# Attention, adapters and a large FFN on one core: the causal mask of the row maxima, split into constant rows and quarter-width products

## The chip, the core and the metric

The kernel runs on one core of a Trainium2 chip. The metric is the time of one execution on the device in microseconds (us), the median of several runs. The core has five engines with a queue of instructions each: TensorE (PE, with its weight loads written PEld), VectorE (DVE), ScalarE (ACT), GpSimd (POOL) and SyncE (SP), which here only issues DMAs. They meet at semaphores alone.

## What is computed

16 sequences of 256 tokens with 256 features go through two residual blocks: x + attention(adapter(x)), and x + ffn(cond2(x)). The change touches the attention only:

```python
q = (x @ Wq.T).reshape(b, t, NUM_HEADS, HEAD_DIM)      # 16 heads of 16
k = x @ Wk.T                                           # one key head for all
v = x @ Wv.T
logits = jnp.einsum('btnh,bsh->bnts', q, k) * scale
mask = (q_pos >= k_pos) & (q_pos <= k_pos + WINDOW)    # WINDOW = 256 >= t
masked = jnp.where(mask[None, None, :, :], logits, -1e30)
probs = jax.nn.softmax(masked, axis=-1)
out = jnp.einsum('bnts,bsh->btnh', probs, v).reshape(b, t, WIDTH)
return out @ Wf.T + bf
```

Softmax subtracts the maximum of each row of `masked`, so the kernel needs, for each query and head, the maximum over the keys up to its own token. After it come an FFN block with experts chosen per sequence and a second, ternary FFN.

## The kernel before

There are three phases: attention (one sequence an iteration, to about 353 us of the trace), the expert FFN, and the ternary FFN, in which PE streams 512-column products without a pause (line 1599). The change is in the attention alone.

**The iteration.** Each engine runs the same list of steps, written out by hand in a function `iteration`, and a loop repeats it. Three sequences are in work at once: while iteration b does scores and exponentials of sequence b, it also does the adapter, norm, queries and keys of sequence b+2 (`front`), the row maxima of sequence b+1 (`maxima`), and the products with the values, the output projection and the residual of sequence b-1 (`tail`). Operands of three sequences lie in three slots: `q_t[slot]` (128 rows x 8 pairs of heads x 256 tokens) and `keys[slot]` (128 rows x 2 x 256). In a slot rows 0 to 63 serve the even head of a pair and rows 64 to 127 the odd one; of the 64, rows 0 to 47 hold the query's high part, rest and high part against the key's high, high and low part, and rows 48 and 49 the row maximum against -1. Rows 50 to 63 are zero on the query side.

**The maxima.** `max_scores(n, slot, u)` makes unit u of the 12 units of a sequence on PE (line 1282 the products of queries and keys, line 1285 the mask), and `maximum` on DVE (line 927) reduces the 512 columns of its bank to the negated maxima. Units 0 to 3 take tokens 0 to 127 and two pairs of heads each (two products of 256 columns, then a mask product of 512 columns); units 4 to 11 take tokens 128 to 255 and one pair (one product of 512 columns, then a mask product of 256 columns, which covers the last 128 keys). The mask product multiplies a bf16 identity of 128 x 128 by a constant bf16 tile with -1e30 above the diagonal and adds it into the bank. Two banks alternate, so unit u waits for the reduction of unit u-2.

**What follows on PE.** Between the units stand the score products (`scores`, line 1301, 512 columns each, read by ACT's exponential, line 624), transposes (1237, 1340, 1347), projections (1248, 1258, 1356), and the adapter (1218, 1228). The exponentials are masked on POOL (`causal`, line 521). The products with the values (`products`, lines 1320 and 1322) have 32 rows of output each: four of them, to output rows 0, 32, 64 and 96 of a bank, stand one behind the other, with fp32 operands, of which the trace has two records per product.

**The end of an iteration.** On DVE: the reductions of units 10 and 11, the split of the maxima (941, 943), the residual (959), then values and low keys (920, 906). On PE: units 10 and 11, the output projection (1356), two transposes of the values (1264), the transposes of the maxima (1290), scores 10 and 11, and then the next iteration's `adapter_in` (1218), whose bank the residual on DVE reads.

**The start.** POOL clears the three `q_t` slots and other constants (lines 495 to 504). SP issues the loads of constants, the first loads of sequence 1 (`load_front(1)`), then `move_queries(0, 0)` (line 321, six DMAs that put the parts of the queries on their rows), and so on.

Of the kernel before, what the change touches and what calls it, by code (L numbers as in the profile page):

```python
# [26 lines left out]
SLOTS = 3  # L27

# [74 lines left out]
def build(nc, x_t, x_tok, lang, expert, cond_w1, cond_w2, cond_vec, w_q, w_kv, w_f, b_f, ident_d, mask_d, key_row_d,  # L103
          fc1_w, fc1_b, fc2_w, fc2_b, exp_w, exp_b, ffn_d, hid_d, ffn_s, out_t):
    ctx = ExitStack()
    with ctx:
# [40 lines left out]
        for name in """  # L147
                warm_made sp_settled pool_settled dve_settled raw_loaded const_loaded ffn_copied ffn_loaded const_made ident_made row_made
                front_loaded hidden_mm hidden_out adapted_mm u_out norm_t_mm norm_t_out q_mm q_hi q_low q_moved kv_mm keys_hi keys_out kv_out v_t_mm values_out
                stats_ready moments_ready veps_ready rstd_ready norm_ready  # L150
                max_mm max_out m2_hi m2_ready max_t_mm max_t_out maxima_moved
                score_mm exp_done masked early_mm early_out late_mm late_out
                pv_t_mm recip_done att_out att_t_mm att_t_out proj_mm x1_out resid_loaded x1_stored
                phase2_over fc1_hi_made fc1_split fc2_loaded fc2_hi_made fc2_split
                xa_loaded xa_hi xa_split expert_loaded expert_hi expert_split bias_loaded
                unit_mm raw_ready hi_ready act_ready y_ready y_stored
                comb_made comb_checked comb_stored low_step bits_max bits_summed flag_ready
                yc_loaded yc_hi yc_split resid2_loaded sil_ready prod_ready in_mm h_mm w3_part out_mm
                op_hi op_ready p1_out t1_ready t2_ready t3_ready t4_ready u2_ready u3_ready
                x11_ready c21_ready x21_ready c22_ready x22_ready c12_ready x12_ready  # L160
                out_ready out_stored""".split():
            s[name] = sem(name)
# [100 lines left out]

        block = ctx.enter_context(nc.Block())
# [22 lines left out]
        def _(sp):  # L287
# [21 lines left out]
            def load_resid(b):  # L309
                if not is_first(b):  # L310
                    sp.wait_ge(s["x1_out"], HEAD + KD * b)
                sp.dma_start(resid[:, :, :], x_t[:, :, bass.ds(b * T, T)]).then_inc(s["resid_loaded"], 16)

# [83 lines left out]
            sp.dma_start(key_row[:, :], key_row_d).then_inc(s["const_loaded"], 16)  # L397
            load_resid(0)
# [5 lines left out]
            sp.wait_ge(s["const_made"], 1)  # L404
            move_queries(0, 0)
            load_front(2)
            sp.wait_ge(s["const_made"], 3)
# [83 lines left out]
        def _(pool):  # L491
# [3 lines left out]
            nc.gpsimd.memset(q_t[0][:, :, :].bitcast(F32), 0.0).then_inc(s["const_made"], 1)  # L495
            nc.gpsimd.memset(half[:, :], -0.5).then_inc(s["const_made"], 1)
            nc.gpsimd.memset(q_t[1][:, :, :].bitcast(F32), 0.0).then_inc(s["const_made"], 1)
            for slot in range(SLOTS):
                nc.gpsimd.memset(values[slot][:, :, :], 0.0).then_inc(s["const_made"], 1)
            pool.wait_ge(s["const_made"], 3 + SLOTS)  # L500
            for slot in range(SLOTS):
                nc.gpsimd.memset(values[slot][:, :, HD:HD + 1], 1.0).then_inc(s["const_made"], 1)
            nc.gpsimd.memset(q_t[2][:, :, :].bitcast(F32), 0.0).then_inc(s["const_made"], 1)
            nc.gpsimd.memset(ones[:, :], 1.0).then_inc(s["const_made"], 1)
# [3 lines left out]
            def rstd_of(n):  # L508
                pool.wait_ge(s["veps_ready"], n + 1)
                if is_first(n):  # L510
                    pool.wait_ge(s["const_made"], 2)
                nc.gpsimd.tensor_tensor(rstd[:, :], veps[:, :], half[:, :], ALU.pow).then_inc(s["rstd_ready"], 1)
# [76 lines left out]
        def _(act):  # L589
# [23 lines left out]
            def keys_high(n, slot):  # L613
                act.wait_ge(s["kv_out"], n + 1)
                for par in range(2):
                    nc.scalar.activation(keys[slot][:, par, :], kv[:, :], ACT.Identity,
                                         bias=key_row[:, 2 * par:2 * par + 1], scale=key_row[:, 2 * par + 1:2 * par + 2]).then_inc(s["keys_hi"], 1)
# [264 lines left out]
        def _(dve):  # L882
# [20 lines left out]
            def keys_low(n, slot):  # L903
                dve.wait_ge(s["keys_hi"], 2 * (n + 1))
                for par, rows in enumerate((slice(32, 64), slice(96, 128))):
                    nc.vector.tensor_tensor(keys[slot][rows, par, :], kv[rows, :], keys[slot][rows, par, :].bitcast(F32),
                                            ALU.subtract).then_inc(s["keys_out"], 1)
# [6 lines left out]
            def values_of(n, slot):  # L914
                dve.wait_ge(s["v_t_mm"], n + 1)
                if n in (0, 1, 2) if isinstance(n, int) else False:
                    dve.wait_ge(s["const_made"], 3 + 2 * SLOTS)
# [134 lines left out]
            dve.wait_ge(s["front_loaded"], 80)  # L1052
            add_adapted(0)
# [154 lines left out]
        def _(pe):  # L1208
# [58 lines left out]
            def max_scores(n, slot, u):  # L1267
# [3 lines left out]
                if u == 0:  # L1271
                    pe.wait_ge(s["q_moved"], 96 * (n + 1))
                    pe.wait_ge(s["keys_out"], 2 * (n + 1))
                    if not is_first(n):
# [10 lines left out]
                mm(diag, ident_b[:, :], mask[:, 0:2 * pairs, :], start=False, stop=True).then_inc(s["max_mm"], 1)  # L1285
# [433 lines left out]
```

## Time and profile before

| | us |
|---|---|
| median of 3 runs | 1143.06 |
| lowest, highest | 1142.23, 1147.89 |
| the profiled execution's own time | 1147.46 |
| its span, first to last instruction | 1145.7 |

All rows come from one profiled execution. A row of a group of instructions gives line, engine, operation, output<-inputs, `weights` shape, the moving operand's shape and type, count, then busy time and the mean duration (ns) of one, and the idle time ahead of them with what ended it. A row of a timeline gives start and length in us, and how many records were merged. A matmul's length holds the way through the array too: the next one starts well before it ends, so the pace of PE is read from the distance between starts. Some mask products have no record (176 of 192).

### The profile page before, as it was taken

To read this page: it belongs to the slowest core of one execution; us is meant where nothing else is said; L and a number is where in the kernel's file an instruction comes from. 1 tells how busy PE (TensorE), PEld (TensorE's weight loads), DVE (VectorE), ACT (ScalarE), POOL (GpSimd) and SP (SyncE) were. 2 spreads that over 40 slices of the span, in tenths; PEclk is the share of its full clock that TensorE was granted. 3 is DMA by queue.
4 is the path that set the end of the run, shared out by engine and by line. 5 is a ranking of instruction groups with operands and counts; after the bars stand their busy time and mean duration, and the time that the engine had idled before them with its cause. 6 is when DMAs were issued, how large, how long until landed. Compare 5 with 4: busy or idle time off the path is not lost.

```text
span 1145.7 us, 17992 instructions
## 1 busy us (share of the span) xinstructions
PE 1103.2 (96%) x5947; PEld 869.3 (76%) x5963; DVE 783.1 (68%) x1377; ACT 589.5 (51%) x990; POOL 173.4 (15%) x192
## 2 busy tenths in 40 slices
PE   5697999999998999999999999999999999999998
PEld 3465777676765888888888888888888888888886
DVE  2565777777776567566487775777757787568875
ACT  1154656565656445434365654656545564455653
POOL 2021222222245443541000000000000000000000
PEclk9688999999999999999999999999999999999999
DMA  4455555546474456545414443144430444404421
GB/s 134 68 150 171 106 101 101 100 101 103 99 205 148 166 200 210 214 174 185 155 41 164 165 147 110 37 165 147 164 111 11 164 142 162 144 0 147 147 92 38
DMA packets 80591, 148.57 MB, mean 130 GB/s; under 512 B 15328, under 2 KB 41840, under 8 KB 80368
## 3 DMA queue, kind: packets, MB, share of 16 engines
q1 hardware_dynamic: 71026, 126.92, 38.8%
q10 hardware_dynamic: 9518, 21.11, 5.2%
q8 instruction: 19, 0.31, 0.1%
q14 instruction: 28, 0.23, 0.1%
HBM read 107.63 MB, written 30.41 MB: 120 GB/s over the span
## 4 chain that ended last, share of the span: by engine, by line
PE 91%; DVE 3%; DMA 1%; ACT 1%; SPq 1%; issue 1%; ACTq 0%; POOL 0%; DVEq 0%; POOLq 0%
PE bank L1599 35%; PE bank L1561 10%; PE bank L1364 7%; PE bank L1611 5%; PE bank L1282 4%; PE bank L1537 4%; PE bank L1531 4%; PE bank L1301 3%; PE bank L1248 3%; PE bank L1320 2%; PE bank L1356 2%; PE bank L1285 2%; PE bank L1218 2%; DMA vec<-in_cond_vec 1%; PE bank L1228 1%; PE bank L1258 1%
## 5 line engine op out<-in xcount | busy, mean ns | idle before, releaser
L1599 PE MATMUL bank<-op_hi,w_ring 128*128 128x512 f32 x896 | 348.7, 389 | 0.0
L1599 PE MATMUL bank<-op_lo,w_ring 128*128 128x512 f32 x896 | 348.6, 389 | 0.0
L1118 DVE TENSOR_TENSOR op_lo<-x_blk,op_hi 128x512 fp32r<-128x512 f32 x288 | 193.4, 683 | 30.4 <-ACT op_hi L805 30.3
L805 ACT ACTIVATE op_hi<-x_blk 128x512 fp32r<-128x512 f32 x288 | 162.8, 620 | 73.5 <-PE bank L1599 69.3
L1599 PEld LDWEIGHTS bank<-op_lo,w_ring 128*128 128x128 f32 x896 | 168.2, 188 | 35.0
L1599 PEld LDWEIGHTS bank<-op_hi,w_ring 128*128 128x128 f32 x896 | 168.1, 188 | 35.0
L927 DVE TENSOR_REDUCE neg_max<-bank 128x2 f32<-128x512 f32 (+1 forms) x192 | 124.8, 684 | 35.7 <-PE bank L1285 34.4
L624 ACT ACTIVATE p<-bank 128x512 f32<-128x512 f32 x192 | 108.7, 596 | 39.0 <-PE bank L1301 34.7
L829 ACT ACTIVATE x_blk<-x_blk,scales 128x512 f32<-128x512 f32 x96 | 69.3, 722 | 67.0 <-DVE x_blk L1171 28.9
L1561 PE MATMUL bank<-tile_hi,ffn_w 128*128 128x512 f32 x256 | 101.6, 397 | 0.0
L1561 PE MATMUL bank<-tile_lo,ffn_w 128*128 128x512 f32 x256 | 100.9, 394 | 0.0
L521 POOL TENSOR_SCALAR_AFFINE_SELECT p<-p 128x512 f32<-128x512 f32 (+1 forms) x96 | 75.9, 791 | 162.6 <-ACT p L624 162.5
L1301 PE MATMUL bank<-q_t,keys 128*128 128x512 f32 x192 | 94.0, 505 | 0.6 <-ACT p L624 0.6
L757 ACT ACTIVATE g_raw<-bank,fc_bias 128x512 f32<-128x512 f32 x64 | 44.0, 689 | 91.8 <-PE bank L1364 77.6
L1282 PE MATMUL bank<-keys,q_t 128*128 128x256 f32 (+1 forms) x256 | 85.9, 392 | 2.6 <-DVE neg_max L927 2.5
L817 ACT ACTIVATE sil<-bank,scales 128x512 f32<-128x512 f32 x64 | 43.9, 688 | 79.2 <-PE bank L1561 79.1
L1126 DVE SCALAR_TENSOR_TENSOR x_blk<-bank,scales,sil 128x512 f32<-128x512 f32 x64 | 48.1, 751 | 51.9 <-PE bank L1561 49.8
L1282 PEld LDWEIGHTS bank<-keys,q_t 128*128 128x128 f32 x256 | 49.7, 199 | 11.1 <-DVE neg_max L927 5.5
L562 POOL TENSOR_TENSOR comb<-comb 128x512 f32<-128x512 f32 x32 | 49.5, 1546 | 56.5 <-DVE g_parts L1084 55.0
L1561 PEld LDWEIGHTS bank<-tile_hi,ffn_w 128*128 128x128 f32 x256 | 48.1, 188 | 11.9
L1561 PEld LDWEIGHTS bank<-tile_lo,ffn_w 128*128 128x128 f32 x256 | 48.2, 188 | 11.2
L1285 PE MATMUL bank<-mask,ident_b 128*128 128x256 bf16 (+1 forms) x176 | 56.6, 322 | 0.0
(126 smaller groups left out, 1741.4 us busy)
## 6 DMA issues: line engine op xcount, KB each, us to landing
w_ring<-hid_scratch SPq DMA_DIRECT2D x112, 512.0 KB, 4.6
hid_scratch<-comb ACTq DMA_DIRECT2D x8, 1792.0 KB, 7.8
q_t<-q_high SPq DMA_DIRECT2D x64, 128.0 KB, 4.9
comb<-in_hid_d ACTq DMA_DIRECT2D x6, 768.0 KB, 5.1
xt<-in_x_t SPq DMA_DIRECT2D x16, 256.0 KB
xtok<-in_x_tok SPq DMA_DIRECT2D x16, 256.0 KB
resid<-in_x_t SPq DMA_DIRECT2D x16, 256.0 KB, 3.0
q_t<-q_rest SPq DMA_DIRECT2D x32, 128.0 KB, 4.6
```

Source lines behind the costliest of these rows:

```text
L521: nc.gpsimd.affine_select(out=v, in_=v, compare_op=ALU.is_ge, fill=0.0, base=0, pattern=[[0, v.shape[1]], [1, P]], channel_multiplier=-1). ...
L624: nc.scalar.activation(dst.rearrange("p c t -> p (c t)"), score_bank[par][:, :], ACT.Exp).then_inc(s["exp_done"], 1)
L805: nc.scalar.activation(op_hi[:, o % OP_RING, k], x_blk[:, operand_home(o), k], ACT.Copy).then_inc(s["op_hi"], 1)
L829: nc.scalar.activation(x_blk[:, at[block], m], src, ACT.Gelu, scale=sc[:, KB * row + m:KB * row + m + 1]).then_inc(s[made], 1)
L927: nc.vector.tensor_reduce(neg_max[:, t, first:first + pairs, :].rearrange("p c a -> p (c a)"), max_bank[u % 2][:, :].rearrange("p (c k) -> ...
L1118: nc.vector.tensor_tensor(op_lo[:, o % OP_RING, k], x_blk[:, operand_home(o), k], op_hi[:, o % OP_RING, k].bitcast(F32), ALU.subtract).the ...
L1282: mm(dst[:, 2 * c * seen:2 * (c + 1) * seen].rearrange("p (a k) -> p a k", a=2), q_t[slot][:, first + c, t * P:(t + 1) * P], keys[slot][:, ...
L1285: mm(diag, ident_b[:, :], mask[:, 0:2 * pairs, :], start=False, stop=True).then_inc(s["max_mm"], 1)
L1301: mm(score_bank[par][:, :].rearrange("p (c t) -> p c t", c=pairs), keys[slot][:, par, k0:k0 + P], q_t[slot][:, first:first + pairs, q0:T], ...
L1364: last = mm(bank, w[:, k, cols], v[:, k, :], start=i == 0, stop=i == len(passes) - 1)
L1561: last = mm(bank, w_at(at, k, HID, m), read(v[:, half, k, :]), start=k == 0 and v is yc_hi, stop=k == KD - 1 and v is yc_lo)
L1599: last = mm(banks[first_bank + m][:, :], w, read(v[:, q % OP_RING, k, :]), start=k == 0 and v is op_hi and i not in (P2, P3), stop=k == KB ...
```

## The change

The mask of the maxima is made in two parts.

Between blocks of 32 tokens: rows 50 to 56 of every `q_t` slot and `keys` slot become seven constant rows. Row r of the queries is 1 where the token's block is below r, row r of the keys is -1e30 where the key's block is r, so the ordinary product of queries and keys adds -1e30 for every key in a later block. They are loaded once (`rank_d`), rounded on DVE and copied into the three slots by six DMAs. POOL clears the `keys` slots too, and `keys_high` (ACT) and `keys_low` (DVE) write no longer over these rows.

Within a block of 32: the one mask product with 128 output rows becomes four, each with 32 weight columns of the identity, 32 output rows, and the 32 keys of that block for each head: 4 x 128 columns for units 0 to 3 (before: 512), 4 x 64 for units 4 to 11 (before: 256). The diff, cut to its core:

```diff
+BLOCK = 32
+RANKS = T // BLOCK - 1
+MASK_ROW = MAX_ROW + 2
...
+        rank_raw, rank = x1[0:RANKS, :, :], att_t[0:RANKS, :, :]
...
+            def move_ranks(slot):
+
+                sp.wait_ge(s["rank_made"], 1)
+                rows = slice(MASK_ROW, MASK_ROW + RANKS)
+                for to, part, count in ((q_t, 0, NP), (keys, 1, 2)):
+                    sp.dma_start(to[slot][rows, :, :].bitcast(F32),
+                                 rank[:, part, :].rearrange("p (c t) -> p c t", c=1).broadcast_to([RANKS, count, T])).then_inc(s["ranks_moved"], 16)
...
             sp.dma_start(key_row[:, :], key_row_d).then_inc(s["const_loaded"], 16)
+            sp.dma_start(rank_raw, rank_d).then_inc(s["rank_loaded"], 16)
             load_resid(0)
...
             load_front(1)
-            sp.wait_ge(s["const_made"], 1)
+            sp.wait_ge(s["const_made"], 7 + 2 * SLOTS)
+            for slot in range(SLOTS):
+                move_ranks(slot)
             move_queries(0, 0)
             load_front(2)
-            sp.wait_ge(s["const_made"], 3)
             move_queries(1, 1)
...
             nc.gpsimd.memset(q_t[0][:, :, :].bitcast(F32), 0.0).then_inc(s["const_made"], 1)
+            nc.gpsimd.memset(keys[0][:, :, :].bitcast(F32), 0.0).then_inc(s["const_made"], 1)
...
                 for par in range(2):
-                    nc.scalar.activation(keys[slot][:, par, :], kv[:, :], ACT.Identity,
-                                         bias=key_row[:, 2 * par:2 * par + 1], scale=key_row[:, 2 * par + 1:2 * par + 2]).then_inc(s["keys_hi"], 1)
+                    rows = slice(SLOT * par, SLOT * par + MASK_ROW)
+                    nc.scalar.activation(keys[slot][rows, par, :], kv[rows, :], ACT.Identity,
+                                         bias=key_row[rows, 2 * par:2 * par + 1], scale=key_row[rows, 2 * par + 1:2 * par + 2]).then_inc(s["keys_hi"], 1)
...
-                for par, rows in enumerate((slice(32, 64), slice(96, 128))):
+                for par, rows in enumerate((slice(32, MASK_ROW), slice(SLOT + 32, SLOT + MASK_ROW))):
...
             dve.wait_ge(s["front_loaded"], 80)
+            dve.wait_ge(s["rank_loaded"], 16)
+            nc.vector.tensor_copy(rank.bitcast(F32R), rank_raw).then_inc(s["rank_made"], 1)
             add_adapted(0)
...
                     pe.wait_ge(s["keys_out"], 2 * (n + 1))
+                    if is_first(n):
+                        pe.wait_ge(s["ranks_moved"], 32 * SLOTS)
...
                 diag = dst[:, :].rearrange("p (h k) -> p h k", k=seen)[:, :, seen - P:seen]
-                mm(diag, ident_b[:, :], mask[:, 0:2 * pairs, :], start=False, stop=True).then_inc(s["max_mm"], 1)
+                for at in range(0, P, BLOCK):
+                    own = slice(at, at + BLOCK)
+                    last = mm(diag[own, :, own], ident_b[:, own], mask[:, 0:2 * pairs, own], start=False, stop=True)
+                last.then_inc(s["max_mm"], 1)
...
+    block, r = np.arange(T) // BLOCK, np.arange(1, RANKS + 1)[:, None]
+    a["rank_d"] = np.stack([np.where(block < r, 1.0, 0.0), np.where(block == r, -1e30, 0.0)], 1).astype(np.float32)
```

On PE, in the loop of the attention, around units 4 to 6 (line 1301 or 1328 is a score product). Before:

```order
L1282 MATMUL bank<-keys,q_t 128x512 [waits max_out]
L1285 MATMUL bank<-mask,ident_b 128x2x128
L1298 REGISTER_ALU
L1301 MATMUL bank<-q_t,keys 128x512 [waits exp_done]
L1279 REGISTER_ALU
L1282 MATMUL bank<-keys,q_t 128x512 [waits max_out]
L1285 MATMUL bank<-mask,ident_b 128x2x128
L1248 MATMUL bank<-norm_t,wq 128x256 [waits late_out,norm_t_out]
```

The same place after the change:

```order
L1306 MATMUL bank<-keys,q_t 128x512 [waits max_out]
L1311 MATMUL bank<-mask,ident_b 32x2x32 x4
L1325 REGISTER_ALU
L1328 MATMUL bank<-q_t,keys 128x512 [waits exp_done]
L1303 REGISTER_ALU
L1306 MATMUL bank<-keys,q_t 128x512 [waits max_out]
L1311 MATMUL bank<-mask,ident_b 32x2x32 x4
L1270 MATMUL bank<-norm_t,wq 128x256 [waits late_out,norm_t_out]
```

The order of the steps stays; one full-width mask product has become four quarter-width ones at every unit.

On SP's queue at the start, behind the loads of sequence 1, before the change:

```order
L301 DMA xtok<-in_x_tok 128x512 [waits u_out,norm_t_out]
L302 ISA
L302 DMA vec<-in_cond_vec 128x5
L321 DMA q_t<-q_high 16x8x256 [waits const_made,q_low]
L321 DMA q_t<-q_high 16x8x256
```

After it:

```order
L307 DMA xtok<-in_x_tok 128x512 [waits u_out,norm_t_out]
L308 ISA
L308 DMA vec<-in_cond_vec 128x5
L325 DMA q_t<-att_t 7x8x256 [waits rank_made,const_made]
L325 DMA keys<-att_t 7x2x256
L325 DMA q_t<-att_t 7x8x256 [waits rank_made]
L325 DMA keys<-att_t 7x2x256
L325 DMA q_t<-att_t 7x8x256 [waits rank_made]
L325 DMA keys<-att_t 7x2x256
L335 DMA q_t<-q_high 16x8x256 [waits q_low]
L335 DMA q_t<-q_high 16x8x256
```

Six DMAs now stand ahead of the queries of sequence 0.

## Rows read from the trace of the kernel before

**Rows 1.** The page: its head, and the group of mask products from its part 5.
```profile
span 1145.7 us, 17992 instructions
...
L1285 PE MATMUL bank<-mask,ident_b 128*128 128x256 bf16 (+1 forms) x176 | 56.6, 322 | 0.0
```

**Rows 2.** Stretches: length; busy of PE, PEld, DVE, ACT, POOL; granted clock; DMA; GB/s.
```profile
40.00:60.00 20.00, 15.62 (x48) 9.12 (x47) 13.80 (x28) 2.62 (x6) 0.33 (x1) 0.67 0.32 42
...
200.00:300.00 100.00, 99.48 (x764) 70.65 (x767) 73.52 (x169) 59.84 (x119) 27.54 (x36) 1.00 0.55 102
```

**Rows 3.** Timeline of PE: the first maxima products of two iterations in a row.
```profile
206.57 0.97 PE L1282 MATMUL bank<-keys,q_t 128*128 128x256 f32 x4
...
226.28 0.97 PE L1282 MATMUL bank<-keys,q_t 128*128 128x256 f32 x4
```

**Rows 4.** Timeline of PE around two mask products of 512 and 256 columns.
```profile
209.64 0.40 PE L1282 MATMUL bank<-keys,q_t 128*128 128x256 f32 x2
...
210.34 0.27 PE L1237 MATMUL bank<-ident,norm 128*128 128x128 f32 x1
...
211.02 0.39 PE L1282 MATMUL bank<-keys,q_t 128*128 128x512 f32 x1
...
211.60 0.39 PE L1282 MATMUL bank<-keys,q_t 128*128 128x512 f32 x1
```

**Rows 5.** Timeline of PE: back-to-back 512-column products of the FFN, first and seventh.
```profile
820.06 0.39 PE L1599 MATMUL bank<-op_hi,w_ring 128*128 128x512 f32 x1
...
821.42 0.39 PE L1599 MATMUL bank<-op_hi,w_ring 128*128 128x512 f32 x1
```

**Rows 6.** Timelines of PE and its weight loads, from full-width products to quarter-width ones and back.
```profile
202.32 0.38 PE L1218 MATMUL bank<-xt,w1c 128*128 128x256 f32 x1
...
202.63 0.16 PEld L1320 LDWEIGHTS bank<-p,values 128*32 128x32 f32 x8 [0.33 <-issue]
...
202.87 0.40 PE L1320 MATMUL bank<-p,values 128*32 128x256 f32 x4
203.09 0.40 PE L1322 MATMUL bank<-p,values 128*32 128x128 f32 x8
203.31 0.40 PE L1320 MATMUL bank<-p,values 128*32 128x256 f32 x4
...
203.86 0.28 PE L1322 MATMUL bank<-p,values 128*32 128x128 f32 x2
...
204.07 0.30 PEld L1228 LDWEIGHTS bank<-w2c,h_t 65*128 65x128 f32 x2 [0.20 <-issue]
...
204.39 0.38 PE L1228 MATMUL bank<-w2c,h_t 65*128 65x256 f32 x1
```

**Rows 7.** The end of an iteration: timelines of DVE, PE, PEld; then L1218's idle by releaser.
```profile
218.18 1.29 DVE L927 TENSOR_REDUCE neg_max<-bank 128x2 f32<-128x512 f32 x2 [0.34 <-PE bank L1285]
...
220.35 0.88 DVE L959 SCALAR_TENSOR_TENSOR x<-bank,bf,resid 128x256 f32<-128x256 f32 x2
...
218.22 0.28 PE L1285 MATMUL bank<-mask,ident_b 128*128 128x256 bf16 x1
...
220.47 0.71 PE L1301 MATMUL bank<-q_t,keys 128*128 128x512 f32 x2
...
221.28 0.51 PEld L1218 LDWEIGHTS bank<-xt,w1c 128*128 128x128 f32 x3 [0.53 <-DVE x L959]
...
  DVE x L959: 5.6, 11
```

**Rows 8.** The start: timelines of DVE, SP's queue (SPq) and POOL.
```profile
14.40 0.69 DVE L886 TENSOR_TENSOR u<-bank,xtok 128x512 f32<-128x512 f32 x1 [12.27 <-PE bank L1228]
...
20.96 0.34 SPq L302 DMA_DIRECT2D vec<-in_cond_vec  x1
25.52 1.31 SPq L321 DMA_DIRECT2D q_t<-q_high  x2
...
5.82 1.80 POOL L503 MEMSET q_t<- 128x2048 f32 x1
```

More of the change, by code:

```diff
@@ L100, in score_fill, with build @@
     return 2 * [0, 1, None, 2, 3][f], 2, 0, 0
-def build(nc, x_t, x_tok, lang, expert, cond_w1, cond_w2, cond_vec, w_q, w_kv, w_f, b_f, ident_d, mask_d, key_row_d,
+def build(nc, x_t, x_tok, lang, expert, cond_w1, cond_w2, cond_vec, w_q, w_kv, w_f, b_f, ident_d, mask_d, key_row_d, rank_d,
           fc1_w, fc1_b, fc2_w, fc2_b, exp_w, exp_b, ffn_d, hid_d, ffn_s, out_t):
@@ L147, in build @@
         for name in """
-                warm_made sp_settled pool_settled dve_settled raw_loaded const_loaded ffn_copied ffn_loaded const_made ident_made row_made
+                warm_made sp_settled pool_settled dve_settled raw_loaded const_loaded rank_loaded rank_made ranks_moved ffn_copied ffn_loaded const_made ident_made row_made
                 front_loaded hidden_mm hidden_out adapted_mm u_out norm_t_mm norm_t_out q_mm q_hi q_low q_moved kv_mm keys_hi keys_out kv_out v_t_mm values_out
@@ L495, in _ @@
             nc.gpsimd.memset(q_t[0][:, :, :].bitcast(F32), 0.0).then_inc(s["const_made"], 1)
+            nc.gpsimd.memset(keys[0][:, :, :].bitcast(F32), 0.0).then_inc(s["const_made"], 1)
             nc.gpsimd.memset(half[:, :], -0.5).then_inc(s["const_made"], 1)
             nc.gpsimd.memset(q_t[1][:, :, :].bitcast(F32), 0.0).then_inc(s["const_made"], 1)
+            nc.gpsimd.memset(keys[1][:, :, :].bitcast(F32), 0.0).then_inc(s["const_made"], 1)
             for slot in range(SLOTS):
                 nc.gpsimd.memset(values[slot][:, :, :], 0.0).then_inc(s["const_made"], 1)
-            pool.wait_ge(s["const_made"], 3 + SLOTS)
+            pool.wait_ge(s["const_made"], 5 + SLOTS)
             for slot in range(SLOTS):
@@ L503, in _ @@
             nc.gpsimd.memset(q_t[2][:, :, :].bitcast(F32), 0.0).then_inc(s["const_made"], 1)
+            nc.gpsimd.memset(keys[2][:, :, :].bitcast(F32), 0.0).then_inc(s["const_made"], 1)
             nc.gpsimd.memset(ones[:, :], 1.0).then_inc(s["const_made"], 1)
@@ L510, in rstd_of @@
                 if is_first(n):
-                    pool.wait_ge(s["const_made"], 2)
+                    pool.wait_ge(s["const_made"], 3)
                 nc.gpsimd.tensor_tensor(rstd[:, :], veps[:, :], half[:, :], ALU.pow).then_inc(s["rstd_ready"], 1)
@@ L916, in values_of @@
                 if n in (0, 1, 2) if isinstance(n, int) else False:
-                    dve.wait_ge(s["const_made"], 3 + 2 * SLOTS)
+                    dve.wait_ge(s["const_made"], 5 + 2 * SLOTS)
                 src, at = ring[1][:, T:2 * T].rearrange("p (t c) -> p t c", t=NT), 0
```

## The prediction

> **What bounds the kernel now.** I read the busy time by stretch first. In a hundred microseconds of the attention PE is busy for 99.5 us at a granted clock of 1.00 (the level of 2.4 GHz), DVE for 73.5 and ACT for 59.8 [rows 2]: PE sets the time there, and what it does less or more shows in the total, unless PE was waiting anyway. Busy time alone hides such waits, because the length of a matmul record holds its way through the array, so I then read the distances between starts in the timeline. One iteration is 226.28 - 206.57 = 19.71 us [rows 3]. The mask products count as 56.6 us busy [rows 1], but that is not what they cost, since their records lie over their neighbours'.
>
> What one costs is in [rows 4]. From one 512-column maxima product to the next stand a product, a mask product of 256 columns and a score product of 512: 211.60 - 211.02 = 0.58 us. Products of 512 columns alone come every (821.42 - 820.06) / 6 = 0.227 us [rows 5]. So the mask product of 256 columns costs 0.58 - 2 x 0.227 = 0.13. For the 512-column mask: 210.34 - 209.64 = 0.70 us for two products of 256 columns (together 0.23), the mask and a score product (0.227), which leaves 0.24. An iteration has 8 of the one and 4 of the other: 8 x 0.13 + 4 x 0.24 = 2.0 us, and 16 sequences 32 us. This is all that the masks can give back.
>
> **The quarter-width products.** The trace has products with 32 output rows to four different quarters of a bank: those with the values. Two things can be read from them [rows 6].
>
> First, four of them run at once. The first pass of four with 128 columns starts at 203.09, the next four with 256 columns at 203.31; between lie two passes of 128 columns for all four quarters, eight records, in 0.22 us, so 0.11 for four. The four with 256 columns before them (202.87 to 203.09) take 0.22, which is what one such fp32 pass takes alone. And four records together last 0.40 us (start 203.31) where one lasts 0.38 (start 202.32): the four starts are spread over 0.02 us.
>
> Second, going in and out is not free. The last full-width pass ahead of the quarters starts at 202.32, and the second round of the quarters at 202.87. At 0.22 us a pass, two passes would be 0.43 us; it is 0.55. **Entering costs 0.12 us.** The weight loader sat idle for 0.33 us before the quarters [rows 6], though its wait was for nothing that the profile shows ("issue"), where elsewhere it loads under the running product. The last round of quarters starts up to 203.86 (two records) and takes 0.11, so it is through at 203.97; the second full-width pass of the next product starts at 204.39, its first one therefore counts from 204.39 - 0.22 = 204.17. **Leaving costs 0.20 us**, again with an idle weight loader (0.20, "issue"). The three other crossings of this iteration that I looked at have the same two distances to the hundredth, so these are no late semaphores but a price of changing between full and quarter width: the running products have to be through before the new weights are loaded, and the load is then uncovered.
>
> The Trainium skill says so too, in "TensorEngine Tiling (Array Packing)", Key Properties: changing the tiling mode drains TensorE. This trace agrees (the loader's 0.33 and 0.20 us), and the page gives no figure for it. Against it stands the span model of "TensorE: Matmul & The Clock Gate", Part 3 (measured speedup vs the span model), by which four tiles take the time of one and about 4 ns for each further one, with no word of a drain; by that rule alone the change would end as the first rival below does.
>
> **The sum.** After the change every unit crosses twice: its query-key product is full width, the four quarters are not, and what follows is full width again. The order of the steps puts no two masks side by side. The streaming of the quarters is small: 256 more bf16 columns cost 0.24 - 0.13 = 0.11, so 64 columns cost 0.03 and 128 columns 0.05, all four at once, and 0.02 for the spread of their starts. A mask then costs
> - units 4 to 11: 0.12 + 0.03 + 0.02 + 0.20 = 0.37, before 0.13: +0.24;
> - units 0 to 3: 0.12 + 0.05 + 0.02 + 0.20 = 0.39, before 0.24: +0.15.
>
> The pace of 0.227 holds some 0.01 beyond the streaming (two fp32 passes of 256 columns take 0.22), and a drain that begins at the end of the stream has it already; I take +0.23 and +0.14. An iteration: 8 x 0.23 + 4 x 0.14 = 2.4 us; 16 sequences: 38.4 us.
>
> **What is given back.** At the end of an iteration PE waits for DVE. Scores 10 and 11 start from 220.47 and, two at 0.227 apart, are through at about 221.0; the next `adapter_in` loads its weights at 221.28, released by the residual on DVE (220.35 + 0.88) [rows 7]. That is about 0.3 us in each of the 13 iterations with a tail that are followed by an adapter; over the trace the row counts 11 such waits with 5.6 us of idle loader. The chain on DVE goes back to unit 10: the reductions of units 10 and 11 start at 218.18, right behind unit 10's mask, and run back to back for 1.29 us [rows 7]; then split and residual. With the change unit 11 comes later by its own crossings and by leaving unit 10's, about 0.4 us on PE, and its reduction moves by about 0.1 only, because it had to wait for unit 10's reduction anyway. So PE arrives some 0.3 us later at a wait that ends some 0.1 us later: the old wait takes up 0.3 us, 13 x 0.3 = 4 us. What is late next is DVE's split and residual by 0.1, and nobody else waits for them.
>
> Other edits cost nothing. The four quarters need no more semaphores. `keys_high` and `keys_low` work on fewer partitions with the same columns. The rounding of the ranks on DVE (7 x 512) falls into the 12.27 us that DVE sits idle before 14.40 [rows 8]. The clearing of `keys` adds 3 x 512 columns on POOL, 3 x 0.45 us by the 1.80 for 2048 columns, and POOL's list then ends near 9 us, long before SP asks for it at 21.3. The six DMAs stand ahead of the queries of sequence 0: at some 0.65 us each (1.31 for two [rows 8]) they take 3.9 us, from 21.3 to 25.2, and SP waited for the queries until 25.52 [rows 8] anyway. Without this cover they would cost 3.9 us, once.
>
> Sum: 38.4 - 4 = 34 us. The profiled execution would go from 1147.5 to 1181.5; it lay 4.4 us above the median of the three runs shown, and from that median it is 1143 + 34 = **1177 us**.
>
> **Rivals.**
> - *No drain at these crossings: faster.* If the gaps of [rows 6] belonged to something else (fp32 operands in two passes, or the waits of those two steps), the four quarters would cost 0.05 or 0.07 us: 8 x 0.08 + 4 x 0.17 = 1.3 us saved an iteration, 21 us in all: 1122 us. For it: no quarter of the trace has a bf16 operand or an fp32r neighbour ahead. Against it: the same distances at each crossing, and on the way out the neighbour is once an fp32 and once an fp32r product. It decides from a crossing price of 0.08 us in and out together; the rows show 0.32. 8 in 100.
> - *The quarters don't overlap and the drain is there.* Streamed one after another, they cost 4 x 0.03 - 0.03 = 0.08 and 4 x 0.05 - 0.05 = 0.16 more: 8 x 0.08 + 4 x 0.16 = 1.3 us an iteration, 21 us: 1198. Against it is the 0.11 for four in [rows 6]. 4 in 100.
> - *The clock.* More gaps on PE could lower its granted clock. The stretch from 40 to 60 us has 0.67 of it with PE busy for 15.6 of 20 us [rows 2]; in the steady part PE would still be busy nearly all the time by its records, with gaps of 0.3 us at most, as today's at the values (clock 1.00). Were a tenth of the 290 us of attention at half clock, it would be 30 us more: 1207. 3 in 100.
> - *It is hidden.* If PE's slack were larger than its rows show, or the start took it up, the time would be within 6 us of 1143. Only some 0.3 us of slack an iteration is to be found. 2 in 100.
>
> **How the numbers follow.** The forecast has the rest, 83 in 100, and its time is 1177. The terms that move it: leaving may cost 0.10 instead of 0.20, if the next product's weights are loaded during the drain (12 x 0.1 x 16 = 19 us less, 1158), and the part given back may be nothing (4 us more); at the reduced clock of the first two sequences a crossing may cost twice (24 x 0.3 = 7 us more); the runs themselves spread by 5 us. The range 1160 to 1194 takes these in and leaves out the rival cases, some 2 in 10. A measurement tells a change of 0.5% (6 us) from none. Faster: 0.08 for the first rival and 0.01 for the unforeseen; same 0.02; slower 0.89.
>
> **What would show it.** In the profile after: the four mask records of a unit start within 0.03 us of each other; the weight loader has an idle gap before them and before what follows them, 12 times each an iteration; from one 512-column maxima product to the next with a score product between is about 0.81 us instead of 0.58; the iteration is about 21.7 us instead of 19.7; the wait for the residual at `adapter_in` is gone or nearly; the start and the ternary FFN stay. The prediction is wrong if these gaps are missing, if the gap behind the quarters is only half, or if PE's granted clock falls in the stretch from 120 to 350 us.

## The result and the profile after

The changed kernel takes 1171.49 us (median of 4 runs, 1170.87 to 1172.05) against 1143.4 (median of 4): ratio 1.0241, 95% interval 1.0216 to 1.0266. It is slower by 28 us; 34 were forecast, 1177 in all. The profiled execution spans 1170.0 us against 1145.7 [rows 1].

The page after, head and the mask's weight loads from part 5, which were too small to be listed there before:

```profile
span 1170.0 us, 19172 instructions
...
L1311 PEld LDWEIGHTS bank<-mask,ident_b 128*32 128x32 bf16 x768 | 19.7, 93 | 53.3 <-issue 45.5
```

The loader is busy for 19.7 us with the quarters' weights and sat idle for 53.3 us ahead of them, 45.5 of it waiting for nothing that the profile shows. That has to be set against the kernel before, where the loader sat idle ahead of the masks' weights too, for 34.0 us:

```profile
L1285 PEld LDWEIGHTS bank<-mask,ident_b 128*128 128x128 bf16 x192 | 18.9, 99 | 34.0 <-issue 29.1
```

So 19.3 us of it are new. The busy time by stretch, which answers to [rows 2]:

```profile
200.00:300.00 100.00, 99.29 (x854) 66.75 (x856) 68.22 (x152) 56.11 (x110) 25.44 (x33) 1.00 0.49 94
```

By this row PE is as busy as before (99.29 of 100 us, clock 1.00). It is the weight loader (66.75 against 70.65), DVE and ACT that fall: they do the same work in more time, and PE's records, which hold the way through the array, cover the drains. The iteration has to be read from starts, as in [rows 3]:

```profile
216.92 0.50 PE L1306 MATMUL bank<-keys,q_t 128*128 128x256 f32 x2
...
238.48 0.50 PE L1306 MATMUL bank<-keys,q_t 128*128 128x256 f32 x2
```

An iteration takes 21.56 us here (21.59 as the mean of many; 19.71 before), so 1.88 more. The timeline of PE at the places of [rows 4]:

```profile
216.92 0.50 PE L1306 MATMUL bank<-keys,q_t 128*128 128x256 f32 x2
217.35 0.24 PE L1311 MATMUL bank<-mask,ident_b 128*32 128x128 bf16 x4
217.52 0.50 PE L1306 MATMUL bank<-keys,q_t 128*128 128x256 f32 x2
...
221.86 0.39 PE L1306 MATMUL bank<-keys,q_t 128*128 128x512 f32 x1
222.17 0.21 PE L1311 MATMUL bank<-mask,ident_b 128*32 128x64 bf16 x4
222.32 0.49 PE L1328 MATMUL bank<-q_t,keys 128*128 128x512 f32 x1
222.65 0.40 PE L1306 MATMUL bank<-keys,q_t 128*128 128x512 f32 x1
```

The four quarters of a unit start together (four records last 0.21 us, and the mean of one is 0.20). From one 512-column product to the next it is now 222.65 - 221.86 = 0.79 us, before 0.58. To see where the 0.21 lie, here are the two records between those of [rows 4], before the change:

```profile
211.25 0.28 PE L1285 MATMUL bank<-mask,ident_b 128*128 128x256 bf16 x1
211.29 0.48 PE L1301 MATMUL bank<-q_t,keys 128*128 128x512 f32 x1
```

From the product to its mask it is 0.31 us instead of 0.23, from the mask to the score product 0.15 instead of 0.04, and from there to the next product 0.33 instead of 0.31. The score product's record lasts 0.49, where 0.39 is the plain length, but that is no news: it lasted 0.48 before.

The end of an iteration in the timelines of DVE and of the weight loads, which answer to [rows 7]:

```profile
230.00 1.29 DVE L947 TENSOR_REDUCE neg_max<-bank 128x2 f32<-128x512 f32 x2 [0.50 <-PE bank L1311]
...
232.56 0.87 DVE L979 SCALAR_TENSOR_TENSOR x<-bank,bf,resid 128x256 f32<-128x256 f32 x2 [0.48 <-PE bank L1383]
...
233.48 0.51 PEld L1240 LDWEIGHTS bank<-xt,w1c 128*128 128x128 f32 x3 [0.57 <-DVE x L979]
```

And the idle time ahead of the adapter's first product (us, times) that the residual ended:

```profile
  DVE x L979: 6.0, 11
```

The wait that was to shrink is still there: 6.0 us over 11 times against 5.6. What DVE's residual waits for has changed: it now sits idle for 0.48 us for PE's output projection.

### The profile page after: what moved, and what is told of

It is laid out like the page before. It is cut to its first block, busy times and chain, and to the rows that moved or that the text cites. A ratio compares the mean times of both kernels' runs of the same rounds, so it can differ in the third digit from the quotient of the medians.

```text
span 1170.0 us, 19172 instructions
## 1 busy us (share of the span) xinstructions
PE 1131.7 (97%) x6539; PEld 877.0 (75%) x6539; DVE 788.3 (67%) x1378; ACT 591.5 (51%) x990; POOL 175.3 (15%) x195
## 3 DMA queue, kind: packets, MB, share of 16 engines
q10 hardware_dynamic: 9518, 21.11, 5.0%
## 4 chain that ended last, share of the span: by engine, by line
PE 91%; DVE 3%; ACT 1%; DMA 1%; SPq 1%; issue 1%; ACTq 0%; POOL 0%; DVEq 0%; POOLq 0%
PE bank L1626 35%; PE bank L1588 10%; PE bank L1391 7%; PE bank L1638 5%; PE bank L1306 4%; PE bank L1328 4%; PE bank L1564 4%; PE bank L1558 4%; PE bank L1270 3%; PE bank L1383 2%; PE bank L1347 2%; PE bank L1311 2%; PE bank L1240 2%; PE bank L1250 1%; PE bank L1280 1%; PE bank L1367 1%
## 5 line engine op out<-in xcount | busy, mean ns | idle before, releaser
L947 DVE TENSOR_REDUCE neg_max<-bank 128x2 f32<-128x512 f32 (+1 forms) x192 | 129.3, 688 | 52.8 <-PE bank L1311 49.0
L1311 PEld LDWEIGHTS bank<-mask,ident_b 128*32 128x32 bf16 x768 | 19.7, 93 | 53.3 <-issue 45.5
```

The costliest lines, as they stand in the source:

```text
L947: nc.vector.tensor_reduce(neg_max[:, t, first:first + pairs, :].rearrange("p c a -> p (c a)"), max_bank[u % 2][:, :].rearrange("p (c k) -> ...
```

## The experiments

All ratios are to the kernel before, run on the same chip; its median was 1145.5 to 1145.8 us in these three groups. It was 1143.4 beside the changed kernel, so a difference of 2 us between times of different groups says little, and against these later runs the changed kernel's 1171.49 is 26 us more, not 28. Times per iteration are the distance between the first maxima products of neighbouring iterations in each trace.

**The rest of the change alone.** The full-width product is put back into the changed kernel.

```diff
-                for at in range(0, P, BLOCK):
-                    own = slice(at, at + BLOCK)
-                    last = mm(diag[own, :, own], ident_b[:, own], mask[:, 0:2 * pairs, own], start=False, stop=True)
-                last.then_inc(s["max_mm"], 1)
+                mm(diag, ident_b[:, :], mask[:, 0:2 * pairs, :], start=False, stop=True).then_inc(s["max_mm"], 1)
```

> The changed kernel with the one full-width mask product back in place of the four quarters; the seven constant rows, their six DMAs, the clearing of the keys and the changed key writes stay (keys in later blocks get the mask twice). Theory (the quarters cost all of the 28 us, the rest of the change is hidden): 1143 us, within 3 of the kernel before, an iteration of 19.7 us. Rival (the constant rows or the DMAs ahead of the first queries cost some of it): 1147 to 1150, with a later first maxima product.

Measured: 1146.49 us, ratio 1.0005 (0.9988 to 1.0022), 19.71 us an iteration. The first theory holds: the constant rows, the clears and the DMAs cost nothing that can be measured. The timeline of SP's queue at the start shows how near that was:

```profile
21.06 1.01 SPq L325 DMA_DIRECT2D q_t<-att_t  x1
22.12 0.83 SPq L325 DMA_DIRECT2D keys<-att_t  x1
...
25.46 0.78 SPq L325 DMA_DIRECT2D keys<-att_t  x1
26.37 1.29 SPq L335 DMA_DIRECT2D q_t<-q_high  x2
```

The six DMAs take 5.3 us, not 3.9, so the queries of sequence 0 leave at 26.37 instead of 25.52 [rows 8]; the first maxima product still starts at 38.7 us (38.6 before), so it was not the queries that it waited for.

**One quarter instead of four.** Only the last quarter is left; the queries of the three other blocks stay unmasked inside their 32 keys.

```diff
-                       keys[slot][:, :, 0:seen], start=c == 0, stop=False)
+                       keys[slot][:, :, 0:seen], start=c == 0, stop=c == pairs - 1)
...
-                for at in range(0, P, BLOCK):
+                for at in range(P - BLOCK, P, BLOCK):
...
```

> The changed kernel with only the last of the four quarter products of each unit; the other three blocks of queries are left unmasked within their 32 keys. Theory (the price is that of the crossings between full and quarter width, once in and once out, whatever stands between): 3 starts of some 3 ns and no column less, so 2 us at most under the changed kernel: 1169 to 1171. Rival (each quarter product has a price of its own): three quarters of some 60 us go, 1125 us.

Measured: 1170.73 us, ratio 1.0226 (1.0193 to 1.0259). Its timeline of PE:

```profile
205.16 0.39 PE L1306 MATMUL bank<-keys,q_t 128*128 128x512 f32 x1
205.48 0.20 PE L1311 MATMUL bank<-mask,ident_b 128*32 128x64 bf16 x1
205.61 0.50 PE L1328 MATMUL bank<-q_t,keys 128*128 128x512 f32 x1
205.95 0.39 PE L1306 MATMUL bank<-keys,q_t 128*128 128x512 f32 x1
```

The unit takes 0.79 us with one quarter as with four. Its iteration is 21.47 us against 21.59, 0.01 a unit. Three of the four products are all but free, and the price is that of going to quarter width and back.

**Halves.** Two products with 64 output rows.

```diff
-                for at in range(0, P, BLOCK):
-                    own = slice(at, at + BLOCK)
+                for at in range(0, P, 2 * BLOCK):
+                    own = slice(at, at + 2 * BLOCK)
```

> Two products with 64 output rows and the 64 keys of their half in place of four with 32. Theory (any change of width drains the array, and the streamed columns double to 128 and 256): 0.03 and 0.05 us more per unit than quarters, 8 x 0.03 + 4 x 0.05 = 0.4 us an iteration, 7 us: 1178. Rival (only quarter width drains): a unit's mask costs 0.07 to 0.12 us, below the full-width one, and the time falls below the kernel before, to 1130 to 1135.

Measured: 1177.95 us, ratio 1.0277 (1.0243 to 1.0312), 22.10 us an iteration, 0.51 more than with quarters where 0.4 was expected. Its timeline of PE:

```profile
205.97 0.39 PE L1306 MATMUL bank<-keys,q_t 128*128 128x512 f32 x1
206.29 0.25 PE L1311 MATMUL bank<-mask,ident_b 128*64 128x128 bf16 x2
```

From the product to its halves it is 0.32 us, as to the quarters (0.31) and not as to the full-width mask (0.23). So half width pays the crossing as quarter width does.

**Quarters for some units only.** Units 0 to 3, or units 4 to 11, the others with the full-width product.

```diff
+                if t == 0:
                     for at in range(0, P, BLOCK):
...
+                else:
+                    last = mm(diag, ident_b[:, :], mask[:, 0:2 * pairs, :], start=False, stop=True)
```

> Quarters for units 0 to 3 only (128 columns each, before: 512); units 4 to 11 have the full-width mask product. By the distances in the changed kernel a quarter group there costs 0.37 us and the 512-column mask cost 0.24; 4 units, of which one is followed by transposes whose weights load faster: 0.4 to 0.5 us an iteration, so 20.15 us, and 1151 to 1152 in all. Rival (few columns against 512 should pay off if the crossing is cheaper after a pair of 256-column products): 1144 or less.

> Quarters for units 4 to 11 only (64 columns, before: 256). By the distances 0.34 against 0.13 us for each of 8 units, so 1.5 to 1.65 us an iteration: 21.2 to 21.4 us, 1167 to 1170 in all. If terms add up, this and the kernel with quarters for units 0 to 3 make 28 us together over the kernel before.

Measured: 1151.67 us, ratio 1.0063 (1.0043 to 1.0083), 20.21 us an iteration (+0.50) for units 0 to 3; 1162.48 us, ratio 1.0160 (1.0124 to 1.0195), 21.11 us (+1.40) for units 4 to 11. The first came out as expected; the second is 0.1 to 0.25 us an iteration and 5 us in all under what was expected. Per iteration the two make 1.90, the whole change 1.88: there the terms add up. In all they make 5.9 + 16.7 = 22.6 us, where 28 was expected (26 against these groups' kernel before); the interval of the second ratio alone is 4 us to either side, so the totals neither show nor refute the sum. Even where 512 columns become 128 a crossing costs more than it saves.

**Two crossings fewer.** The quarters of units 0 and 1 stand together behind both units' products, and those of 10 and 11 too.

```diff
+                if u in (1, 11):
+                    max_mask(u - 1)
+                if u not in (0, 10):
+                    max_mask(u)
...
```

> The changed kernel with the quarters of units 0 and 1 together behind both units' full-width products, and those of 10 and 11 too: two crossings in and two out fewer per iteration. Theory (a pair of crossings costs 0.30 us on PE, and PE sets the time): 2 x 0.30 x 16 = 9.6 us less than the changed kernel, 1162; if the later mask of unit 10 delays DVE's last two reductions (0.2 us later) and with them the end of the iteration, half of that: 1166. Rival (the gaps beside the quarters come from something else, such as the first small product waiting for the bank): no change, 1171.

Measured: 1166.51 us, ratio 1.0200 (1.0168 to 1.0231), 21.28 us an iteration, 0.31 less than the changed kernel, and 5 us in all (by the ratios alone the two intervals just overlap): the case with half of it lost. Its waits from 200 to 300 us (who waited, for whom, us in total, times, longest) show where the other 0.3 went; neither row stands among those of the changed kernel:

```profile
PEld bank L1306 <- DVE neg_max L947: 2.1, 10, 0.2
PEld bank L1325 <- DVE m L963: 1.1, 5, 0.2
```

PE is through sooner and waits for DVE, whose reductions begin later: 3.2 us of idle loader in 4.7 iterations, of which a part lies under running products.

**No products inside the blocks.** The seven constant rows alone; a row's maximum then runs over up to 31 later tokens. The softmax is the same with any larger number subtracted, but for rounding and for underflow where later keys score far above the row's own.

```diff
-                       keys[slot][:, :, 0:seen], start=c == 0, stop=False)
...
-                for at in range(0, P, BLOCK):
-                    own = slice(at, at + BLOCK)
-                    last = mm(diag[own, :, own], ident_b[:, own], mask[:, 0:2 * pairs, own], start=False, stop=True)
...
+                              keys[slot][:, :, 0:seen], start=c == 0, stop=c == pairs - 1)
                 last.then_inc(s["max_mm"], 1)
```

> The changed kernel without any product inside the blocks: the seven rows alone mask the maxima, so a row's maximum runs over up to 31 later tokens too; the exponentials are still masked, and the softmax is the same but for rounding. Theory: the masks of the kernel before cost 2.0 us an iteration and the quarters 3.9, so this takes 2.0 us an iteration off the kernel before: 1111 us, iteration 17.7 us, or 60 us under the changed kernel. Rival (with less on PE, DVE's reductions set the pace of the units): the iteration stays above 18.5 us, 1125 or more, with PE idle before the maxima products for DVE.

Measured: 1134.21 us, ratio 0.9904 (0.9872 to 0.9936), 18.94 us an iteration. The theory fell here, by 23 us: I had taken the 2.0 us that the masks occupy on PE for what their absence gives, and only 0.77 came. Its waits from 200 to 300 us:

```profile
PEld bank L1306 <- DVE neg_max L947: 4.5, 16, 0.3
...
PEld bank L1270 <- ACT norm_t L616: 2.3, 6, 0.4
...
PEld bank L1259 <- DVE norm L920: 1.5, 6, 0.3
```

These three make 8.3 us of idle loader in 5.3 iterations, 1.6 us each, where the kernel before had only the one for ACT, 0.9 us in the same stretch. PE was the bound, but with other engines close behind it. The rival holds in its iteration (above 18.5), its time (above 1125) and its mechanism, PE idle ahead of the maxima products for DVE, with the waits for the norm on DVE and ACT beside it.

**No mask and no constant rows, and two orders of it.** The kernel before without mask products on the maxima; a row's maximum runs over the keys to the end of its tile of 128.

```diff
-                diag = dst[:, :].rearrange("p (h k) -> p h k", k=seen)[:, :, seen - P:seen]
-                mm(diag, ident_b[:, :], mask[:, 0:2 * pairs, :], start=False, stop=True).then_inc(s["max_mm"], 1)
...
+                last.then_inc(s["max_mm"], 1)
```

> The kernel before with no mask on the maxima at all, and without the constant rows: a row's maximum runs over all keys up to the end of its 128-token tile, later ones too; the exponentials are still masked, so the softmax stays the same but for rounding. Theory (the constant rows cost nothing, and the gain is capped by PE's waits for DVE at 18.94 us an iteration): as with the rows alone, 1134, 0.990 of the kernel before. Rival (the rows' DMAs or clears cost some): 1130 to 1132.

Measured: 1134.47 us, ratio 0.9901 (0.9874 to 0.9928), 18.94 us an iteration, as with the seven rows. One of its six executions took 3741 us; the ratio is without it, there is no trace of it, and it stays unexplained. Then score product 9 was moved, between units 10 and 11, or behind the output projection:

> The same without the late score product: score 9 between units 10 and 11, so that no two units stand side by side on PE at the end. Theory (PE waits for DVE's reduction before units that stand closer than 0.6 us): the 0.2 us wait ahead of unit 11 goes, 18.75 us an iteration, 1131. Rival (it only moves to the transposes of the maxima, which wait for DVE's split): 18.94, 1134.

> The kernel before without any mask on the maxima (they run over later tokens of the tile too) and with score product 9 behind the output projection. Theory: the wait at the end of the iteration shrinks by 0.2 us, but unit 10 and 11 come closer behind unit 9, and DVE's reductions lag by up to 0.2: 18.7 to 18.9 us an iteration, 1131 to 1134. Rival (DVE's reductions set the pace there): 18.94 or more, 1134 to 1137.

Measured: between the units 1132.88 us, ratio 0.9882 (0.9865 to 0.9900), still 18.93 us an iteration; behind the projection 1138.72 us, ratio 0.9943 (0.9928 to 0.9957), 19.09 to 19.6. The first is the fastest version found, but its iteration is that of the others, and its interval overlaps theirs. Its timelines of the weight loads and of DVE:

```profile
210.51 0.19 PEld L1282 LDWEIGHTS bank<-keys,q_t 128*128 128x128 f32 x1 [0.31 <-DVE neg_max L927]
...
208.49 3.24 DVE L927 TENSOR_REDUCE neg_max<-bank 128x2 f32<-128x512 f32 x5
...
212.96 0.88 DVE L959 SCALAR_TENSOR_TENSOR x<-bank,bf,resid 128x256 f32<-128x256 f32 x2 [0.78 <-PE bank L1355]
```

The wait ahead of unit 11 did not go: it is 0.31 us with the two units apart, as it is side by side. DVE runs the last five reductions back to back, so the wait does not hang on how close the units stand, and the theory is out; the rival has the time about right and not the place, since no wait moved to the transposes of the maxima. The order behind the projection is slower than both its cases said; PE waits there for the exponentials (2.4 us in ten waits from 200 to 300 us, against 0.8 in five). Which of the steps between ACT, DVE and PE sets 18.93 us stays open.

**The wait at the end of an iteration.** Score product 9 behind the projection in the changed kernel.

```diff
-                if softmax:
-                    scores(b, slot, 9)
                 if maxima:
                     max_scores(b + 1, ahead, 10)
                     max_scores(b + 1, ahead, 11)
                 if tail:
                     project_out(b - 1, front)
+                if softmax:
+                    scores(b, slot, 9)
```

> The changed kernel with score product 9 moved on PE from before unit 10 to behind the output projection. Theory (the wait at the end of an iteration is a chain PE's projection, DVE's residual, PE's next adapter, so it goes along with PE and nothing was given back there by making the units longer): the projection comes 0.23 us earlier while PE's work between it and the adapter grows by 0.23, the wait shrinks from 0.38 to some 0.1 us, the iteration from 21.59 to 21.35 us, 1168 in all. Rival (the wait's end is set by DVE's chain from unit 10's mask, as the prediction had it): unit 10 comes 0.23 earlier too, so this rival expects some gain as well, but with DVE's residual not waiting for the projection; what tells them apart is what the residual waits for: PE's projection (theory) or nothing but DVE's own split.

Measured: 1175.25 us, ratio 1.0259 (1.0241 to 1.0278): 4 us more than the changed kernel by the times, though the intervals of the two ratios overlap; its iteration is 21.75 us in the mean against 21.59. Both theories expected a gain, and there is none. The mechanism can still be read in its timelines of DVE and PE:

```profile
231.53 0.88 DVE L979 SCALAR_TENSOR_TENSOR x<-bank,bf,resid 128x256 f32<-128x256 f32 x2 [0.82 <-PE bank L1383]
...
232.67 1.11 PE L1240 MATMUL bank<-xt,w1c 128*128 128x256 f32 x4
```

And in its waits from 200 to 300 us:

```profile
PEld bank L1328 <- ACT p L644: 1.6, 5, 0.3
PEld bank L1250 <- ACT h_t L611: 1.1, 4, 0.4
```

The residual waits for the projection, longer than before, as the theory said, and no wait of PE for the residual is left among the waits. But ACT gets its scores late and all at once, and PE now waits for the exponentials and for `h_t` on the same engine; some iterations take 21.67 and some 21.9 us.

## Why the prediction came out right, and what in it was wrong

**The crossing sets the time: right, and shown.** With one quarter in place of four the unit keeps its 0.79 us and the kernel its 1171; with the full-width product back it is the kernel before. The rival without a drain (1122) and the one with quarters streamed one after another (1198) are out, and so is the clock: its granted value is 1.00 in every stretch from 120 to 400 us. The Trainium skill's sentence in "TensorEngine Tiling (Array Packing)", Key Properties, that a change of tiling mode drains TensorE, agrees with the 0.08 and 0.11 us more on the two sides of the quarters, and with the halves, which it covers too. The span model of "TensorE: Matmul & The Clock Gate", Part 3, agrees for the quarters among themselves: the one and the four end within a hundredth. The drain stands around them.

One sign did not come as written. The prediction wanted an idle gap of the weight loader before the quarters and another before what follows them, and called itself wrong if they were missing. The loader's timeline of the changed kernel:

```profile
222.17 0.10 PEld L1311 LDWEIGHTS bank<-mask,ident_b 128*32 128x32 bf16 x4 [0.36 <-issue]
222.31 0.19 PEld L1328 LDWEIGHTS bank<-q_t,keys 128*128 128x128 f32 x1
```

The gap ahead is there (0.36). Behind it is 222.31 - 222.27 = 0.04 us, because the four loads themselves fill that time. The price of leaving still shows in the distances: by the pace of 0.227 the score product behind can be put at 222.65 - 0.23 = 222.42 (an estimate), 0.25 us behind the start of the quarters, where 0.03 of streaming, 0.02 of spread and 0.20 of leaving were forecast. Entering cost 0.08 where 0.12 was forecast.

**The size of the term: 2.4 us an iteration forecast, 1.88 measured.** (The prediction's remark that two fp32 passes of 256 columns take 0.22 us is a slip; by its own rows it is one pass, and two take 0.43.) A quarter group of 64 columns adds 0.79 - 0.58 = 0.21 (forecast 0.23). For 128 columns, 217.52 - 216.92 = 0.60 less two products of 256 columns (0.23) is 0.37 against 0.24 before: 0.13 (forecast 0.14). So 8 x 0.21 + 4 x 0.13 = 2.2. Two more things make it 1.9. Behind units 1 and 9 come transposes, whose weights load faster (in the trace their first record lasts 0.33 us where the others last 0.27, so 0.06 is uncovered instead of 0.10), 0.1 us. And a cover that I had overlooked: ahead of the query projection PE waited for ACT's normalised input, as the waits of the kernel before show from 200 to 300 us, and after the change that row is gone:

```profile
PEld bank L1248 <- ACT norm_t L597: 0.9, 5, 0.2
```

That is 0.18 us of idle loader an iteration. The distance from unit 5's product, over the query projection, to unit 6's shows it too. The two products of unit 6, before and after:

```profile
213.75 0.59 PE L1282 MATMUL bank<-keys,q_t 128*128 128x512 f32 x1
...
224.76 0.58 PE L1306 MATMUL bank<-keys,q_t 128*128 128x512 f32 x1
```

It was 213.75 - 211.60 = 2.15 us and is 224.76 - 222.65 = 2.11, where every other unit of this kind grew: 0.21 were added, and 0.25 given back. This is arithmetic from the traces; no experiment took this cover away by itself.

**The step that failed is "What is given back"**, 4 us at the end of the iterations. The prediction had the wait start at unit 10's mask and run through DVE's reductions. It did, before, but the output projection ended at almost the same time, and the projection stands on PE behind unit 11, so it moved with every crossing. The two reductions start 0.57 us behind unit 10's product before and 0.58 after, so DVE's chain did not stretch. But from their start to the residual it was 220.35 - 218.18 = 2.17 us and is 232.56 - 230.00 = 2.56: the residual moved by the 0.4 of the two units' crossings on PE. The residual changed its releaser (from its own engine to the projection, 0.48 us), and the wait stayed: 5.6 us before, 6.0 after. The prediction had checked the chain on DVE for its delay and not the second input of the same instruction.

**The start.** The first three sequences were put at 2.4 us each, 7 in all. In the two traces the fourth set of maxima products starts at 108.0 and at 109.0 us, so only 1.0 shows. The adapter's product ahead of it tells why, before and after:

```profile
100.64 2.07 PE L1218 MATMUL bank<-xt,w1c 128*128 128x256 f32 x4 [7.18 <-DMA vec<-in_cond_vec]
...
101.16 2.07 PE L1240 MATMUL bank<-xt,w1c 128*128 128x256 f32 x4 [3.46 <-DMA vec<-in_cond_vec]
```

PE waits there for the load of `vec`. It comes to this wait 4.2 us later than before, at 97.7 instead of 93.5, and leaves it 0.5 later, so 3.7 us were hidden in it. With the full-width product put back into the changed kernel the wait is 6.85 again. (Of the 4.2 us, 0.7 lie ahead of the first maxima product; the granted clock of that execution was 0.70 from 0 to 20 us, against 1.00 before.) The prediction charged these crossings in full and did not look for a wait behind them.

From the fourth set to the last the two traces differ by 22.4 us, and behind the last by 0.9: with the 1.0 these are the 24.3 by which the spans differ. The medians differ by 28, because the profiled execution of the kernel before lay 4 us above its median.

So 8 us were charged too much for the crossings (16 x 0.5), 4 us were given back where nothing was, and 3.7 us of wait at the start were overlooked: 16 x 1.88 - 3.7 = 26 us, where the medians say 28, or 26 against the later runs of the kernel before. The 4 us wrongly given back make good a part of the other two errors, and that is luck. What is not luck is that the crossing's price, by far the largest term, was read from the trace.

## What to carry to other kernels

Before a product is cut into narrower ones, look at what stands on either side of it: a run of quarter-width products (such as the values', 32 records between two crossings) carries the 0.3 us of going in and out, a single group between full-width products does not. Price a removed piece of work not by the time that it occupies on the busiest engine but up to the next wait: 2.0 us of masks an iteration were worth 0.77. And of an instruction that ends a wait, check all inputs, since the one that is early today takes over when the other moves.

## What the runs showed of the hardware

- Leaving quarter width costs more than entering: 0.20 and 0.12 us around the fp32 products of the values, and about 0.20 (an estimate: 0.25 us from the quarters' start to the next product less 0.05 for the quarters) and 0.08 around bf16 quarters of 64 columns.
- Half width (64 output rows) pays the crossing too: 0.32 us from the product to its halves, 0.31 to quarters, 0.23 to a full-width mask.
- PE's busy share hides it: 99.29 of 100 us at clock 1.00 while every iteration lost 1.9 us. The weight loader shows some of it, with 53.3 us idle ahead of the masks' weights against 34.0 before; the price itself is in the distances between starts.
- A narrow output alone is no crossing: the transposes of the maxima (line 1317) have 32 weight columns and stand between full-width products. In the timeline of PE of the changed kernel the two transposes ahead of them, with 128 weight columns, take 232.50 - 232.28 = 0.22 us, 0.11 each and nothing for entering; behind them the score product's record begins after 0.14 us, as before the change (0.15). The single quarter of the experiment above did cross; it is a plain product with bf16 operands to output rows 96 to 127, and which of these differences decides is not shown:

```profile
232.28 0.38 PE L1286 MATMUL bank<-ident,kv 128*128 128x128 f32 x2
232.50 0.38 PE L1317 MATMUL bank<-ident,m 128*32 128x128 f32 x2
232.64 0.71 PE L1328 MATMUL bank<-q_t,keys 128*128 128x512 f32 x2
```
